# Causal attention with 16 heads on one core: the output projection from float32r parts, two splits on GpSimd, and another place for the normalization

## What is computed

```
qk = x @ W_attn + b_attn; q, k = halves of qk; v = x          # per head
y  = causal_attn(q, k, v)                                      # softmax(q k^T / 4, masked) v
e  = v[1:] - y[:-1]; k2 = x[:-1] @ W_k2 + b_k2; q2 = q[1:]
y2 = causal_attn(q2, k2, e), with a row of zeros ahead
x1 = layernorm(x + proj(y) + proj(y2))                         # proj(t) = t @ W_proj + b_proj
x2 = layernorm(x1 + mixture_of_8_experts(x1))                  # experts change batch 0 alone
```

## Time and profile before

| | |
|---|---|
| time, median of 3 runs | 2360.48 us (2355.31 to 2364.48) |
| the profiled execution: its time, its span | 2360.84 us, 2359.1 us |
| granted TensorE clock, mean | 0.992 of full |
| TensorE busy (matmuls) | 2297.3 us, 97% |
| VectorE busy | 2070.3 us, 88% |
| ScalarE busy | 1789.1 us, 76% |
| GpSimd busy | 1558.7 us, 66% |
| the chain that ended last, by engine | TensorE 86%, ScalarE 5%, issue 2%, GpSimd 2%, DMA 2% |
| L809, output projection | x512 records, 127.2 us busy |
| L613, copy of y | x64, 39.0 us |

### The profile page before, as it was taken

How to read it: one execution, slowest core, us unless ns; L and a number is a source line. 1 busy time by engine, 2 the same in 40 slices (tenths; PEclk the granted TensorE clock), 3 DMA queues, 4 the chain that set the end, 5 groups by cost and what they waited for, 6 DMA issues and landing times.

```text
span 2359.1 us, 64991 instructions
## 1 busy us (share of the span) xinstructions
PE 2297.3 (97%) x19670; PEld 1321.2 (56%) x19670; DVE 2070.3 (88%) x9178; ACT 1789.1 (76%) x3456; POOL 1558.7 (66%) x2471
## 2 busy tenths in 40 slices
PE   6999999999999999999999999999999999999997
PEld 4555555555555555555555555555555555555454
DVE  5889999999999999999999899999999999999655
ACT  3577778887877788778777877877778778777753
POOL 4467766666767666776776667776666777776442
PEclk9899999999999999999999999999999999999999
DMA  7555555555555555556555556555565556555111
GB/s 120 91 88 107 105 97 102 103 99 110 107 106 106 95 108 101 98 108 116 104 97 100 102 99 112 106 109 103 97 111 97 98 110 114 105 97 91 57 50 58
DMA packets 171909, 235.09 MB, mean 100 GB/s; under 512 B 26280, under 2 KB 87344, under 8 KB 171568
## 3 DMA queue, kind: packets, MB, share of 16 engines
q1 hardware_dynamic: 170608, 229.37, 53.0%
q10 hardware_dynamic: 960, 1.57, 0.5%
HBM read 58.34 MB, written 17.30 MB: 32 GB/s over the span
## 4 chain that ended last, share of the span: by engine, by line
PE 86%; ACT 5%; issue 2%; POOL 2%; DMA 2%; DVE 1%; SPq 1%; ACTq 0%; POOLq 0%; DVEq 0%
PE out_t L675 26%; PE score_t L714 23%; PE misc L779 13%; PE score L725 9%; PE out_t L753 6%; PE misc L809 5%; ACT heads_t L596 4%; PE score L867 2%; PE misc L746 2%; SPq L385 1%; DMA stack_q<-neg_l 1%; PE score L883 1%; PE misc L792 1%; DMA stack_q<-part_l 1%; POOL prob L456 0%
## 5 line engine op out<-in xcount | busy, mean ns | idle before, releaser
L931 DVE CUSTOM_DVE_ANT_0 junk<-score,mask_rows 128x384 bf16<-128x384 f32 (+3 forms) x3584 | 1681.8, 516 | 197.4 <-PE score L725 190.4
L570 ACT ACTIVATE prob<-score_t 128x512 f32<-128x512 f32 x2560 | 1359.7, 597 | 229.8 <-PE score_t L714 225.4
L456 POOL TENSOR_SCALAR_AFFINE_SELECT prob<-prob 128x512 f32<-128x512 f32 (+1 forms) x1280 | 713.1, 562 | 600.4 <-ACT prob L570 552.3
L714 PE MATMUL score_t<-stack_q,stack_k 50*128 50x128 f32 (+5 forms) x4096 | 975.3, 358 | 12.1 <-DVE max_cols L931 5.5
L725 PE MATMUL score<-stack_k,stack_q 48*128 48x512 f32 (+3 forms) x4096 | 973.2, 348 | 2.7 <-DMA stack_q<-part_l 1.5
L714 PEld LDWEIGHTS score_t<-stack_q,stack_k 50*128 50x128 f32 (+1 forms) x4096 | 609.0, 186 | 543.9 <-ACT prob L570 304.9
L675 PE MATMUL out_t<-prob,value 128*17 128x512 f32 (+3 forms) x8192 | 657.0, 439 | 0.0
L725 PEld LDWEIGHTS score<-stack_k,stack_q 48*128 48x128 f32 x4096 | 614.5, 188 | 24.8 <-DVE max_cols L931 9.4
L931 DVE DVE_READ_ACCUMULATOR2_ANT max_cols<- 128x1 f32 x4096 | 341.2, 83 | 0.0
L675 PEld LDWEIGHTS out_t<-prob,value 128*17 128x17 f32 x8192 | 184.7, 97 | 210.5 <-issue 128.0
L486 POOL TENSOR_TENSOR part_l<-part_f,part_h 128x512 fp32r<-128x512 f32 x192 | 245.6, 1279 | 16.3
(11 more groups left out here) (99 smaller groups left out, 1731.4 us busy)
## 6 DMA issues: line engine op xcount, KB each, us to landing
stack_k<-part_h SPq DMA_DIRECT2D x512, 128.0 KB, 4.3
stack_k<-part_l SPq DMA_DIRECT2D x256, 128.0 KB, 5.2
stack_q<-part_h SPq DMA_DIRECT2D x248, 128.0 KB, 4.1
x_full<-x_turned SPq DMA_DIRECT2D x32, 512.0 KB, 13.7
x_in<-L_attn_x SPq DMA_DIRECT2D x32, 512.0 KB, 5.3
layer_out<-x_in SPq DMA_DIRECT2D x32, 512.0 KB, 5.4
stack_q<-part_l SPq DMA_DIRECT2D x124, 128.0 KB, 5.1
x_next<-L_attn_x SPq DMA_DIRECT2D x32, 384.0 KB
```

Of the source, the lines that this page charges most:

```text
L456: e.affine_select(out=view, in_=view, compare_op=ALU.is_ge, fill=0.0, base=-unit_parts(unit)[1], pattern=[[0, runs], [0, cut], [1, P]], ch ...
L570: e.activation(prob[pair % RING][:, slot % 2 * 512:slot % 2 * 512 + 512], score_t[time % KEY_DEPTH][:, :], ACT.Exp, scale=1.0 / np.sqrt(HE ...
L714: done = e.matmul(score_t[now % KEY_DEPTH][:, col:col + n], keys[rows, pair, kb * P:(kb + 1) * P], stack_q[b % 2][rows, pair, kb * P:token ...
L931: e.tensor_tensor_reduce(junk[count % JUNK][:, 0:n], score[number % MAX_DEPTH][:, col:col + n], mask, 1.0, -3e38, ALU.add, ALU.max, max_co ...
```

## The change

- **Output projection.** `wp` becomes two float32r parts, split once by GpSimd at 7/4 ahead of the first batch; `y_t` becomes two float32r parts. One float32 product (two records) becomes three float32r products, high by high, high by low, low by high.
- **Copy of y.** ScalarE copies the turned half from `misc` to `heads_t` instead of `y_t`, after the transposes of the same slot have read `heads_t` (`s_turned`). GpSimd splits `heads_t` at 1/7 and 2/7, behind that slot's mask; the next copy of sums into `heads_t` waits for it.
- **Maxima.** ScalarE makes one negated copy, `neg_f`; GpSimd casts it to `neg_h` and subtracts to `neg_l`. SyncE issues the two rows of the high part when the cast is done. TensorE's later users of `misc` wait for ScalarE's copy alone.
- **Normalization.** It is due at 1/6, 2/6, 3/6 and 4/6, the store at 4/9, and the load of `x_in` at 5/5 instead of 5/9.
- **Buffers.** `y_sum` and `part_f` are single.

```diff
-         ... "apply": ((8, 8), (11, 5), (12, 4), (13, 2)), "store": ((13, 4),)}
+         ... "apply": ((9, 6), (10, 6), (11, 6), (12, 6)), "store": ((12, 9),)}
...
-                if (place, slot) == (5, 9) and 2 <= b < batches:
+                if (place, slot) == (5, 5) and 2 <= b < batches:
...
-                        e.wait_ge(s_negl, 2 * b + a + 1)
                         for part, tile in enumerate((neg_h, neg_l)):
+                            e.wait_ge(s_negl, 2 * (2 * b + a) + part + 1)
...
-                        e.tensor_tensor(neg_l[:, :], neg_l[:, :].bitcast(F32), neg_h[:, :].bitcast(F32), ALU.subtract).then_inc(s_negl, 1)
+                        if m:
+                            e.wait_ge(s_maxrow[1 - a], 16 * MAX_PARTS * SIDES * (b + a))
+                        e.tensor_copy(neg_h[:, :], neg_f[:, :]).then_inc(s_negl, 1)
+                        e.wait_ge(s_negl, 2 * m + 1)
+                        e.tensor_tensor(neg_l[:, :], neg_f[:, :], neg_h[:, :].bitcast(F32), ALU.subtract).then_inc(s_negl, 1)
...
+                for hf in range(halves):
+                    if (place, slot) == ((1, 7), (2, 7))[hf] and 0 <= ahead - 1 < batches:
+                        b = ahead - 1
+                        e.wait_ge(s_yt, halves * b + hf + 1)
+                        if b:
+                            e.wait_ge(s_proj, 2 * b)
+                        e.tensor_copy(y_t[HIGH][:, hf, :], heads_t[:, :]).then_inc(s_ysplit, 1)
+                        e.wait_ge(s_ysplit, 2 * (halves * b + hf) + 1)
+                        e.tensor_tensor(y_t[LOW][:, hf, :], heads_t[:, :], y_t[HIGH][:, hf, :].bitcast(F32), ALU.subtract).then_inc(s_ysplit, 1)
...
+                        e.tensor_copy(wp[HIGH][:, :, :], wp_full[:, :, :]).then_inc(s_wpsplit, 1)
+                        e.wait_ge(s_wpsplit, 1)
+                        e.tensor_tensor(wp[LOW][:, :, :], wp_full[:, :, :], wp[HIGH][:, :, :].bitcast(F32),
+                                        ALU.subtract).then_inc(s_wpsplit, 1)
...
-                    if n >= 2:
-                        e.wait_ge(s_split, 2 * (n - 1))
-                    e.activation(part_f[n % 2][:, :], misc[:, :], ACT.Identity, ...)
+                    if n:
+                        e.wait_ge(s_split, 2 * n)
+                    e.activation(part_f[:, :], misc[:, :], ACT.Identity, ...)
...
+                    if place in (2, 3) and ahead >= 1:
+                        e.wait_ge(s_ysplit, 2 * (halves * (ahead - 1) + place - 1))
                     e.activation(heads_t[:, :], out_t[:, :], ACT.Identity, bias=sum_floor[:, 0:1]).then_inc(s_heads, 1)
...
-                        e.activation(neg_h[:, :], misc[0:64, 0:P], ACT.Copy, scale=-1.0)
-                        e.activation(neg_l[:, :].bitcast(F32), misc[0:64, 0:P], ACT.Copy, scale=-1.0).then_inc(s_negh, 1)
+                            e.wait_ge(s_negl, 2 * m)
+                        e.activation(neg_f[:, :], misc[0:64, 0:P], ACT.Copy, scale=-1.0).then_inc(s_negh, 1)
...
-                        e.activation(y_t[:, hf, :], misc[:, :], ACT.Copy).then_inc(s_yt, 1)
+                        if halves * b + hf:
+                            e.wait_ge(s_ysplit, 2 * (halves * b + hf))
+                        e.wait_ge(s_turned, min(unit, end))
+                        e.activation(heads_t[:, :], misc[:, :], ACT.Copy).then_inc(s_yt, 1)
...
                         for c in range(halves):
-                            done = e.matmul(misc[:, j * width:(j + 1) * width], y_t[:, c, t * P:(t + 1) * P], wp[:, c, :],
-                                            start=(c == 0), stop=(c == halves - 1))
+                            for i, (py, pw) in enumerate(zip(PARTS_Q, PARTS_K)):
+                                done = e.matmul(misc[:, j * width:(j + 1) * width], y_t[py][:, c, t * P:(t + 1) * P], wp[pw][:, c, :],
+                                                start=(c == 0 and i == 0), stop=(c == halves - 1 and i == TERMS - 1))
```

More of the change, by code:

```diff
@@ L101, in build_layer @@
         wk2 = [sb(f"wk2_{part}", [P, halves, halves, P], F32R) for part in "hl"]
-        wp = sb("wp", [P, halves, width])
+        wp = [sb(f"wp_{part}", [P, halves, width], F32R) for part in "hl"]
         bias_qk = sb("bias_qk", [P, 3 * halves])
@@ L120, in build_layer @@
         x_next = sb("x_next", [P, blocks, width])
-        y_sum = [sb(f"y_sum{i}", [P, blocks, width]) for i in range(2)]
+        y_sum = sb("y_sum", [P, blocks, width])
         y_second = [sb(f"y_second{i}", [P, blocks, GROUP, HEAD_DIM]) for i in range(2)]
-        y_t = sb("y_t", [P, halves, tokens])
+        y_t = [sb(f"y_t_{part}", [P, halves, tokens], F32R) for part in "hl"]
         x_full_at = nc.sbuf_base
@@ L127, in build_layer @@
         heads_t = sb("heads_t", [P, tokens])
-        part_f = [sb(f"part_f{i}", [P, tokens]) for i in range(2)]
+        part_f = sb("part_f", [P, tokens])
         part_h = [sb(f"part_h{i}", [P, tokens], F32R) for i in range(2)]
@@ L158, in build_layer @@
         s_maxrow = [sem(f"s_maxrow{i}") for i in range(2)]
[L160 removed]
+        s_const, s_empty, s_ones, s_bias, s_wsplit, s_wpsplit = (
+            sem(f"s_{n}") for n in ("const", "empty", "ones", "bias", "wsplit", "wpsplit"))
         s_filled = [sem(f"s_filled{i}") for i in range(4)]
@@ L171, in build_layer @@
             sem(f"s_{n}") for n in ("max", "negl", "value1", "floor", "rden", "normal", "attended", "stats", "aggr"))
-        s_mask, s_split, s_xsplit, s_value2, s_added, s_biased, s_ln = (
-            sem(f"s_{n}") for n in ("mask", "split", "xsplit", "value2", "added", "biased", "ln"))
+        s_mask, s_split, s_xsplit, s_ysplit, s_value2, s_added, s_biased, s_ln = (
+            sem(f"s_{n}") for n in ("mask", "split", "xsplit", "ysplit", "value2", "added", "biased", "ln"))
         s_fin, s_fbias = sem("s_fin"), sem("s_fbias")
@@ L517, in _ @@
                     chans = slice(g * GROUP * HEAD_DIM, (g + 1) * GROUP * HEAD_DIM)
-                    y = y_sum[b % 2][:, :, chans].rearrange("p t (h d) -> p t h d", d=HEAD_DIM)
+                    y = y_sum[:, :, chans].rearrange("p t (h d) -> p t h d", d=HEAD_DIM)
                     e.wait_ge(s_normal, done + 1)
@@ L568, in _ @@
                         e.wait_ge(s_pv, GROUP * u + (1, 1, 3, 3, 4)[k])
+                    if pair == 0:
+                        e.wait_ge(s_wpsplit, 2)
                     e.wait_ge(s_key, time + 1)
@@ L579, in _ @@
                         e.wait_ge(s_wq, 32)
-                    if n >= 2:
-                        e.wait_ge(s_split, 2 * (n - 1))
-                    e.activation(part_f[n % 2][:, :], misc[:, :], ACT.Identity, bias=bias_qk[:, column:column + 1]).then_inc(s_full, 1)
+                    if n:
+                        e.wait_ge(s_split, 2 * n)
+                    e.activation(part_f[:, :], misc[:, :], ACT.Identity, bias=bias_qk[:, column:column + 1]).then_inc(s_full, 1)
                 ended = time - 7
@@ L772, in _ @@
                     if place == 7 and ahead + 1 >= 0:
-                        e.wait_ge(s_negl, 2 * ahead + 3)
+                        e.wait_ge(s_negh, 2 * ahead + 3)
                     for c in range(halves):
@@ L797, in _ @@
                     b, pair = now_due
-                    if b == 0 and pair == 0:
-                        e.wait_ge(s_wproj, 32)
-                    e.wait_ge(s_yt, halves * (b + 1))
+                    e.wait_ge(s_ysplit, 2 * halves * (b + 1))
                     e.wait_ge(s_full, min(N_PIECES * (b + 2) + (6 if pair else 4), N_PIECES * batches))
@@ L948, in _ @@
                         e.wait_ge(s_added, GROUPS * b + g - 1)
-                    elif not a and g == 0 and b >= 2:
-                        e.wait_ge(s_yt_pe, halves * (b - 1))
+                    elif not a and b:
+                        e.wait_ge(s_yt_pe, halves * (b - 1) + g // (GROUPS // halves) + 1)
                     e.tensor_tensor(y_second[g % 2][:, :, :, :] if a else y, heads[:, :, :, 0:HEAD_DIM], wide, ALU.mult).then_inc(s_normal, 1)
```

23 lines of the change are left out of this document (11 added, 12 removed).

## The result

The changed kernel takes 2372.09 us (median of 11 runs, 2365.53 to 2379.79) against 2359.29 (11 runs, 2352.01 to 2364.48): ratio 1.006, 95% interval 1.0044 to 1.0075. The forecast was 2368 us in 2334 to 2388; the time lies in the range. The ratio is just beyond the 0.5% that counted as no change, and its interval has that limit inside.

A forecast was written before the change was run, and what follows sets the result against it. Places of a 68 us batch have different limits, with TensorE tied to ScalarE and VectorE. Per batch -0.10 - 0.18 - 0.12 + 0.12 + 0.50 = +0.22 us, times 31 is +6.8: 2368 us, range 2334 to 2388.

The forecast's parts named there:

- The signs it named: Profile signs: projection 1.6 us, value products 0.95 into place 1, neg_h issue 5.1 into place 3, maxima wait some 0.5.
- Part 1: Projection from parts in places 3 and 6: stretch from 1.93 to 1.59 us, a gain of 0.34 us on TensorE.
- Place 6: -0.10: In place 6 only 0.10 us of the projection's 0.34 gets through, because VectorE is behind TensorE there.
- The rival with open weight loads: Weight loads open ahead of the twelve projection products: stretch 2.79 us, 1.66 us slower per batch, 2412 us; chance 0.05.
- Part 2: Normalization moved: -0.18 us in place 1, -0.12 in place 5, 0 in places 3 and 4.
- Part 3: y through heads_t, split by GpSimd: GpSimd enters place 3 0.95 us late; value products lose 0.12 in place 2.
- loss of 0.12 in place 2 and 0.12 in place 3: Value products wait for GpSimd's late mask, 0.12 us in each of the two places, bounds 0 and 0.3.
- Part 4: Negated maxima in place 3: rows issued 0.80 us later, landing no longer hidden, place 0.4 longer, +0.50 with scatter.
- Estimate 0.1 per batch on top: Place 3: upward scatter of the maxima's issues and landings, no longer taken by slack, adds 0.1 us per batch.
- Part 5: Single y_sum and part_f, store and load of x_in, weight split at the start, tail: no cost, 0 us.
- the same wait, larger: Maxima's rows end place 3 later still, with cast 0.45 and masks waited for 0.3 each: 2384 us; chance 0.28.
- GpSimd's delay reaches nobody: Maxima still land in time and the mask is not waited for: 0.74 us gained per batch, 2338 us; chance 0.22.

The follow-up runs named there:

- full_in_change: The changed kernel with the projection's twelve products of parts replaced by four full products, low parts left out: 2367.2 us, ratio 1.004 to the kernel before.
- proj_only: The changed kernel with normalization and maxima as before, leaving the projection from parts and the y split: 2360.7 us, ratio 1.001 to the kernel before.
- norm_skip2: The changed kernel with one normalization step put back from place 2, slot 6 to place 0, slot 8: 2345.7 us, ratio 0.996 to the kernel before.
- norm_only: The kernel before with only the normalization steps, the store and the load of x moved as in the change: 2353.1 us, ratio 0.998.
- max_second: The changed kernel with GpSimd's maxima split at slot 0 of place 3, behind the projected tile's split: 2337.5 us, ratio 0.992 to the kernel before.

## Why the prediction was right, and by how much it was off

The mechanism was the right one: the maxima's rows decide the end of place 3, the projection's gain there is lost to them, and the rest about cancels. The signs it named came: twelve products in 1.6 us, value products 0.96 us into place 1, first issue at 4.99, a wait of 0.57 us ahead of unit 4 in a batch on time. Point by point:

- **Part 1.** Stretch 1.61 us, forecast 1.59. In place 3 the gain is worth nothing (full_in_change), as said. "Place 6: -0.10": TensorE gains 0.26 there and VectorE takes 0.16 back in place 7, in proj_only against before and again in full_in_change against the change; in proj_only the third score pair of place 7, the one that needs VectorE's bank, starts 0.69 us into the place instead of 0.58, and all behind it 0.16 later. Right, as a net of both places. The rival with open weight loads is dead: the twelve products over all rows are 0.12 us apart. By the Trainium skill (TensorE: Matmul & The Clock Gate, Part 3) a weight load overlaps a running matmul only when its row group differs, which would have left these loads open; the trace disagrees.
- **Part 2.** Place 1 gave -0.14 for -0.18, from the step at 0/8, as norm_skip2 shows. Place 5 gave -0.22 for -0.12, but place 6 takes 0.16 of it back, which had no term: net -0.06. It is again the third score pair, 0.69 us into place 6 instead of 0.57 in norm_only.
- **Part 3.** The cover ahead of the copy was underrated: in the mean exponentials behind it start 0.09 later, not 0.18, and that of slot 7 0.57, not 0.67. GpSimd enters place 3 0.83 late, not 0.95 (its last mask starts 1.01 us into the place, 0.18 in the earlier trace rows). The 1.93 us for the split is 1.97 by its own terms (0.61 + 0.08 + 1.28); the trace has 1672.91 - 1670.97 = 1.94. The "loss of 0.12 in place 2 and 0.12 in place 3" for a late mask did not come: place 2 takes 8.43 us in both kernels. The term is 0, its lower bound. Only the 0.12 of place 2 was in the sum; in place 3 it would have passed behind the landing.
- **Part 4.** Cast 0.284 us, forecast 0.30. First issue 0.68 later, forecast 0.80. Place 3 +0.30 in its most frequent length (9.04 for 8.74), forecast +0.4. Up to here the sum would be -0.14 (place 1) + 0.30 (place 3) - 0.22 (place 5) - 0.085 (place 6, mean) + 0.13 (place 7, mean), about 0 per batch.
- **The term that was mis-sized** is "Estimate 0.1 per batch on top" for scatter. I took the spread of landings of the kernel before and let it pass through, 0.1 us. Measured: the mean of place 3 is 0.43 over its most frequent length, against 0.13 before, so 0.30; and place 4, in which I had no term at all, is 0.19 longer in the mean from four stretches of half clock (1.22 + 1.26 + 1.44 + 1.36 = 5.3 us of the 12.8). Against that, 0.12 for the mask of place 2, 0.1 in place 3 and 0.1 in place 5 were forecast too high, and places 6 and 7 together came out 0.15 worse. So a forecast of +6.8 us met +12.8 in the profiles; that it came so near is in part luck. The rival "the same wait, larger" is about as near to this result: the wait did come out larger, 27.8 us over 29 times, but by scatter, not by the cast and the masks that it named.
- **Part 5.** 0 holds: all that lies ahead of the third and behind the thirtieth batch is 0.1 us shorter together.

The rival "GpSimd's delay reaches nobody", 2338 us, describes max_second: 2337.5. Two instructions' place in a queue lay between it and the forecast.

## What to carry to other kernels

Before an engine takes over work, find the step in its queue whose result leaves by DMA and is waited for last, and place that step as early as its input allows; an in-order queue delays it by all that was added ahead, less the gaps there were. A gap absorbs only once: an edit that was free, or a gain, beside one neighbour costs its full length beside another, so edits that share a queue are priced together. When a wait loses its slack, price not only its typical length but the late landings, and what an idle TensorE may lose on its clock afterwards.
